# 64-wide cross attention in rounds of four steps, and tables ahead of stores in two 16-wide cross attentions

## The chip, the cores and the metric

The kernel runs on one core of one Trainium2 chip, as one launch. The metric is the device time in microseconds (us) of that core. The profile is one execution recorded by the hardware profiler. Its engines are TensorE (PE, its weight loads PEld), VectorE (DVE), ScalarE (ACT), GpSimd (POOL) and SyncE (SP), which issues the DMAs.

## The reference

Four Perceiver layers act on x (2 x 256 x 256) with a context of 2 x 4096 x 256. Each has a cross attention to the context, a self attention and a feed-forward part. The change touches the cross attentions of layers 1, 2 and 3.

```python
# layer 1: 16 heads of 64, keys and values from context and latents
q = lat @ Wq
k, v = jnp.split(jnp.concatenate([x, lat], axis=1) @ Wkv, 2, axis=-1)
attn = jax.nn.softmax(jnp.einsum('bhid,bhjd->bhij', q, k) * scale, axis=-1)
out = jnp.einsum('bhij,bhjd->bhid', attn, v)      # then @ Wout
# layers 2 and 3: 16 heads of 16
q, k, v = query @ Wq.T + bq, key @ Wk.T + bk, value @ Wv.T + bv   # split in heads, softmax as above, then @ Wo.T + bo
```

## The kernel before

Each part is a stage with a hand-written instruction list for each engine; semaphores are the only link between them. P is 128, S is 256 queries, KC and QT are 2.

**The 64-wide attention** (`latent_attention`, tiles `L1x_...`). A unit is two heads of one batch (16 units), and has 17 steps of 256 keys (34 key tiles of 128). Two steps are a pair: 136 pairs, `for p in range(PAIRS)`. A softmax needs the row maximum first, so one key tile of 512 keys and one value tile is computed per pair, some pairs ahead of its use. The PE list of a pair is

1. `first_peaks`: score products in bf16 of one key tile into banks 0 and 1 of `psm` (L1525);
2. `scores` of two steps onto banks of `pss` that hold the negated maximum already (L1542);
3. `second_peaks` into banks 1 and 2 (L1525), after DVE has read the first;
4. `tiles`: a key tile into bank 0 (L1501, L1504 for the latent's own keys), a value tile into bank 2 (L1516);
5. in 7 pairs the queries of the next group (L1482), in 15 a row of maxima spread over the partitions (`spread_rows`, L1531);
6. `average` of the two steps (L1555), and at a unit's end `denominators` (L1565).

Peaks and scores use half the array's rows (64*128 in the profile, two of them at once), tiles the whole array (128*128), averages and denominators half its columns (128*64, again two at once). So PE changes its shape three times in a pair.

The ACT list of a pair is two exponentials (L1671), two seeds that copy the maxima into `pss` (L1661), the key's copy (L1646) and the value's (L1650). DVE reads the peaks (L1730, L1733 for the latent's own), sums half of the exponentials for the denominators (L1760) and, where a unit's last peaks are in, builds the diagonal matrices of its maxima (`diagonals`, L1742 and L1747). These stand between the peaks and the sums. At a unit's end it copies the average out (`copy_out`, L1769) and normalizes (L1773, L1775). POOL sums the other half (L1464) and casts the key tile to bf16 (L1450).

**The 16-wide attentions** (`narrow_attention`, tiles `L2x_...` and `L3x_...`, 8 units each) open with a phase that PE, DVE and the DMAs share: the 64 peak tiles of unit 0 (PE L1063 by `products`, read one bank at a time by DVE at L1234) and 16 value tiles of the context (`first_values`, L1131), which ACT copies out (L1205) and SP stores (L1012) and loads again (L980). PE waits for `wv_here` ahead of the first value tile. That semaphore takes three DMAs: the weights `wv` (L997) and, behind the context's first four blocks (L990) and the stores of the query parts (L1002) in SP's list, the tables `bv` and `sel` (L1003, L1004). Then come 12 peaks of unit 1, and the unit loop with scores (L1106) and averages (L1118), which need the keys `KS` (L976) and the values `V` (L980).

## Time and profile before

| | us |
|---|---|
| median of 3 runs | 3573.69 |
| lowest, highest | 3572.43, 3589.18 |
| the profiled execution | 3585.08 |
| its span, first to last instruction | 3583.3 |
| PE, DVE, ACT, POOL busy | 3318.9, 2164.6, 1772.7, 877.4 |
| 64-wide attention (L1x), key tiles to the last denominators | 604 to 1710 |
| 16-wide attentions, start of the first peaks | 2184 (L2x), 2847 (L3x) |

The profiled execution took 11.39 us more than the median of the runs; 1.78 us of its time lie outside its span. All positions in the trace are from the span's start. A matmul's end is modelled, so PE looks busy while it changes shape; what such a change costs is seen in the distance between the starts of two groups, not in the busy time.

### The profile page before, as it was taken

Reading aid. Unit: us, or ns where it says so; the run is one execution under the profiler, and the core shown is the slowest. Engines: PE = TensorE matmul, PEld = TensorE weight load, DVE = VectorE, ACT = ScalarE, POOL = GpSimd, SP = SyncE. Lnnn points to the kernel's source line nnn. Section 1 sums busy time; section 2 is a strip of 40 time slices with the busy share of each in tenths; the row PEclk is TensorE's granted clock in tenths of the full one; section 3 lists DMA queues with packets and bytes.
Section 4 is the critical chain, followed back from the end, with each engine's and each line's share of the span. In section 5 each row is a group of like instructions: output and inputs, shape, how many; then the busy total and the mean of one; then the engine's idle time right before and its main releaser. Section 6 shows DMA issues by size and latency. Waiting matters only on the chain. (4 is left out here: it accounts for less than half of the span.)

```text
span 3583.3 us, 56143 instructions
## 1 busy us (share of the span) xinstructions
PE 3318.9 (93%) x21894; PEld 2109.8 (59%) x21894; DVE 2164.6 (60%) x3410; ACT 1772.7 (49%) x2589; POOL 877.4 (24%) x652
## 2 busy tenths in 40 slices
PE   8989898999999999999769798999988799999899
PEld 5855596666666666666436585444456544445665
DVE  4435313666666666665488405999663299984654
ACT  2325311566666666667356231677743147675621
POOL 1033000344444444445147103000030300000530
PEclk9999999999999999999889899999999999999999
DMA  5258554000001000000586426766201576650010
GB/s 190 101 176 270 198 216 160 1 10 10 1 32 35 1 10 10 1 1 1 139 308 236 158 111 181 150 120 120 49 27 37 173 180 125 120 104 23 1 70 17
DMA packets 231028, 346.79 MB, mean 97 GB/s; under 512 B 104304, under 2 KB 177712, under 8 KB 226160
## 3 DMA queue, kind: packets, MB, share of 16 engines
q1 hardware_dynamic: 230384, 342.16, 32.9%
q8 instruction: 178, 2.92, 0.3%
q0 software_dynamic: 384, 1.05, 0.1%
q14 instruction: 82, 0.67, 0.1%
HBM read 257.15 MB, written 86.02 MB: 96 GB/s over the span
## 5 line engine op out<-in xcount | busy, mean ns | idle before, releaser
L1464 POOL TENSOR_TENSOR L1x_acc<-L1x_acc,L1x_pr 128x512 f32<-128x512 f32 x256 | 357.6, 1397 | 538.6 <-ACT L1x_pr L1671 521.4
L1730 DVE TENSOR_REDUCE L1x_pk<-L1x_psm 128x2 f32<-128x1024 f32 x238 | 291.7, 1226 | 318.9 <-PE L1x_psm L1525 318.9
L1671 ACT ACTIVATE L1x_pr<-L1x_pss 128x1024 f32<-128x1024 f32 x272 | 263.7, 1021 | 300.6 <-PE L1x_pss L1542 300.5
L1234 DVE TENSOR_REDUCE L3x_pk<-L3x_psm 128x1 f32<-128x512 f32 x512 | 328.9, 685 | 23.7 <-PE L3x_psm L1063 17.3
L1234 DVE TENSOR_REDUCE L2x_pk<-L2x_psm 128x1 f32<-128x512 f32 x512 | 329.0, 685 | 23.0 <-PE L2x_psm L1063 16.6
L1211 ACT ACTIVATE L3x_pr<-L3x_pss 128x1024 f32<-128x1024 f32 x256 | 248.1, 1021 | 104.1 <-PE L3x_pss L1106 103.8
L1211 ACT ACTIVATE L2x_pr<-L2x_pss 128x1024 f32<-128x1024 f32 x256 | 248.1, 1021 | 103.0 <-PE L2x_pss L1106 102.7
L1760 DVE TENSOR_TENSOR L1x_acc<-L1x_acc,L1x_pr 128x512 f32<-128x512 f32 x256 | 275.1, 1075 | 33.5 <-ACT L1x_pr L1671 21.0
L1661 ACT COPY L1x_pss<-L1x_neg 128x1024 f32<-128x1024 f32 x272 | 278.5, 1028 | 1.3 <-DVE L1x_pk L1730 1.3
L1555 PE MATMUL L1x_pso<-L1x_pr,L1x_V 128*64 128x256 f32 x2176 | 265.3, 386 | 2.6 <-ACT L1x_pr L1671 2.6
L1501 PE MATMUL L1x_psm<-L1x_cT,L1x_w 128*128 128x512 f32 x512 | 253.4, 618 | 0.0
L1542 PE MATMUL L1x_pss<-L1x_Q,L1x_K 64*128 64x256 f32 x2048 | 244.3, 377 | 0.7 <-ACT L1x_pss L1661 0.7
L1516 PE MATMUL L1x_psm<-L1x_w,L1x_cT 128*128 128x256 f32 x1024 | 242.0, 379 | 1.3 <-DVE L1x_pk L1730 1.3
L1516 PEld LDWEIGHTS L1x_psm<-L1x_w,L1x_cT 128*128 128x128 f32 x1024 | 194.5, 190 | 79.0 <-issue 30.2
L3016 POOL TENSOR_SCALAR s_qz<-s_qT,s_mask 128x256 f32<-128x256 f32 x64 | 58.3, 920 | 657.3 <-SPq L58 437.6
L1542 PEld LDWEIGHTS L1x_pss<-L1x_Q,L1x_K 64*128 64x128 f32 x2048 | 194.5, 188 | 27.2 <-ACT L1x_pss L1661 3.7
L1555 PEld LDWEIGHTS L1x_pso<-L1x_pr,L1x_V 128*64 128x64 f32 x2176 | 143.4, 136 | 107.1 <-issue 40.7
L3998 POOL TENSOR_TENSOR o_pr<-o_h,m_cr 128x1024 f32<-128x1024 f32 x31 | 72.8, 2354 | 504.2 <-DVE o_h L4077 504.2
L841 PE MATMUL n_psk<-n_cT,n_w 128*128 128x512 f32 x256 | 126.2, 618 | 36.1 <-DMA n_cT<-in_ctxT 36.0
L1501 PEld LDWEIGHTS L1x_psm<-L1x_cT,L1x_w 128*128 128x128 f32 x512 | 87.0, 189 | 113.1 <-issue 112.8
L879 ACT ACTIVATE n_kst<-n_psk,n_b 128x512 bf16<-128x512 f32 x192 | 121.6, 688 | 57.6 <-PE n_psk L841 47.4
L1106 PE MATMUL L2x_pss<-L2x_QS,L2x_KS 97*128 97x256 bf16 x1024 | 138.1, 277 | 0.6
(747 smaller groups left out, 5881.0 us busy)
## 6 DMA issues: line engine op xcount, KB each, us to landing
f0e_wt<-in_f_pieces SPq DMA_DIRECT2D x10, 3072.0 KB, 11.5
offset_rows<-s_rows SPq DMA_DIRECT2D x32, 768.0 KB, 5.7
L2x_KS<-L2x_key_parts SPq DMA_DIRECT2D x24, 1024.0 KB, 12.9
L3x_KS<-L3x_key_parts SPq DMA_DIRECT2D x24, 1024.0 KB, 12.8
s_add<-offset_rows SPq DMA_DIRECT2D x32, 512.0 KB, 7.3
n_cT<-in_ctxT SPq DMA_DIRECT2D x32, 512.0 KB, 4.8
f1e_wt<-in_f_pieces SPq DMA_DIRECT2D x8, 2048.0 KB, 13.2
L2x_key_parts<-n_kst SPq DMA_DIRECT2D x32, 384.0 KB, 3.0
```

The source lines that it names most:

```text
L1106: i = nc.tensor.matmul(pss[:, 2 * (a % 2) + h // 2, h % 2 * S:(h % 2 + 1) * S], KS[0:ONE + 1, n % 2, h, s * P:(s + 1) * P], QS[0:ONE + 1, ...
L1211: nc.scalar.activation(pr[:, a % RING, :, :].rearrange("p h q -> p (h q)"), pss[:, 2 * (a % 2):2 * (a % 2) + 2, :].rearrange("p x q -> p ( ...
L1234: nc.vector.reduce_max(pk[:, n % 2, h * QT + qt, j:j + 1], psm[:, x % 3, :], AX).then_inc(turn_read, 1)
L1464: i = nc.gpsimd.tensor_tensor(acc[:, n, 1, :, :], acc[:, n, 1, :, :], pr[:, a % RING, :, 1, :], ALU.add)
L1501: i = nc.tensor.matmul(psm[:, x, :], w[:, g % 2, 1, c, m * P:(m + 1) * P], cT[:, c, j * 512:(j + 1) * 512], start=(c == 0), stop=(c == KC ...
L1516: i = nc.tensor.matmul(psm[:, 2, h * D:(h + 1) * D], keys, w[:, g % 2, 2, c, :], start=(c == 0), stop=(c == KC - 1))
L1542: i = nc.tensor.matmul(pss[:, 2 * (a % 2) + h, e * S:(e + 1) * S], keys, Q[half, g % 2, m, :], start=False, stop=True, skip_group_check=True)
L1555: i = nc.tensor.matmul(pso[64 * h:64 * h + 64, 0:S], V[:, (SLOTS * g + s) % VRING, e, 2 * n + h, :], pr[:, a % RING, h, e, :], start=(s == ...
L1661: nc.scalar.copy(pss[:, x:x + 2, :].rearrange("p h (e q) -> p h e q", e=2), neg[:, u % 2, :, :].unsqueeze(2).broadcast_to([P, 2, 2, S])).t ...
L1671: nc.scalar.activation(pr[:, a % RING, :, :, :].rearrange("p h e q -> p (h e q)"), pss[:, x:x + 2, :].rearrange("p h n -> p (h n)"), ACT.E ...
L1730: nc.vector.reduce_max(pk[:, m, qt, :, j], peak_banks(z, qt), AX).then_inc(peak_read, 1)
L1760: i = nc.vector.tensor_tensor(acc[:, n, 0, :, :], acc[:, n, 0, :, :], pr[:, a % RING, :, 0, :], ALU.add)
```

## The change

- **64-wide, PE.** Pairs are taken two at a time, as 68 rounds of four steps. `visit(p)` is peaks, two steps' scores, peaks; `fill(p)` is the pair's tiles. A round is `visit(2r)`, the tiles of both pairs, `visit(2r+1)`, and then four averages: those of steps 4r-2 to 4r+1. In the 10 rounds in which a unit ends ahead of the round's last step, the averages up to that end stand ahead of the tiles. In rounds without tiles (the last four) two averages follow each visit. Waits for a bank of `psm` are gathered in `bank0_free`, `bank1_free` and `bank2_free`, with counters.
- **64-wide, the others.** ACT, DVE and POOL do the work of the tiles (copies, queries, rows, casts, the end of a unit) in the even pair of the round. DVE's `diagonals` stay with the visit whose peaks complete a unit, ahead of the sums, in the even or the odd pair. One more key tile is computed ahead (`KLEAD` 12 for 11); the rings of exponentials and of values grow by two (`RING` 6, `VRING` 21). The tile `dn` goes; `rec` takes its place.
- **16-wide, peaks of unit 0.** `first_products` writes two banks and `read_first_peaks` reads both in one instruction (1024 columns for 512). The two rooms are banks 0 and 1 of `psm` and of `pss`. Four products stand ahead of one whole value tile, where two stood ahead of each half.
- **16-wide, SP.** `bv` and `sel` are issued right behind `wv`, ahead of the context's blocks and the query parts.

```diff
+        def wide_banks(x):
+            return psm[:, 0:2, :] if x % 2 == 0 else pss[:, 0:2, :]
...
             sp.dma_start(wv[:, :, :], d[pre + "_w3"][0][:, 2]).then_inc(wv_here, 16)
+            sp.dma_start(bv[:, :], d[pre + "_bvT"]).then_inc(wv_here, 16)
+            sp.dma_start(sel[:, :], d["sum_rows"]).then_inc(wv_here, 16)
             for j in range(CRING):
...
-            sp.dma_start(bv[:, :], d[pre + "_bvT"]).then_inc(wv_here, 16)
-            sp.dma_start(sel[:, :], d["sum_rows"]).then_inc(wv_here, 16)
...
+            def first_products(x):
+                if x == 0:
+                    pe.wait_ge(kh_in[0], 32)
+                    pe.wait_ge(masked, 2)
+                if x == 1:
+                    pe.wait_ge(q_act, 3 * KC)
+                if x >= 2:
+                    pe.wait_ge(wide_read, x - 1)
+                j, qt, h = peak_of(2 * x)
+                for r in range(2):
+                    i = nc.tensor.matmul(wide_banks(x)[:, r, :], QM[64 * r:64 * r + 64, 0, h, qt * P:(qt + 1) * P],
+                                         KH[64 * r:64 * r + 64, 0, j * 512:(j + 1) * 512], start=True, stop=True)
+                i.then_inc(wide, 1)
...
             for n in range(NV):
-                products(0, n * NP // NV, (2 * n + 1) * NP // NV // 2)
+                first_products(2 * n)
+                first_products(2 * n + 1)
                 if n == 0:
                     for i in range(2, 2 * NU):
                         picked(i)
                     pe.wait_ge(masked_more, NU - 1)
                     pe.wait_ge(wv_here, 48)
                 first_values(n, 0)
-                products(0, (2 * n + 1) * NP // NV // 2, (n + 1) * NP // NV)
                 first_values(n, 1)
             products(1, 0, LATE)
             rows(0)
...
+            def read_first_peaks(x):
+                j, qt, h = peak_of(2 * x)
+                dve.wait_ge(wide, x + 1)
+                nc.vector.reduce_max(pk[:, 0, h * QT + qt::2 * QT, j], wide_banks(x), AX).then_inc(wide_read, 1)
+                if x == NP // 2 - 1:
...
-    KLEAD, VLEAD, VRING, BRING = 11, 9, SLOTS + 2, 3
+    KLEAD, VLEAD, VRING, BRING = 12, 9, SLOTS + 4, 3
+    ROUNDS = ALL // 4
...
-            g, r = divmod(p, SLOTS)
-            return KC * g if r == 9 else KC * g - 1 if r == 0 and g else None
-        def averages_in(p):
-            r = p % SLOTS
-            return [2 * p] if r == 8 else [2 * p - 1, 2 * p, 2 * p + 1] if r == 9 else [2 * p, 2 * p + 1]
+            u = [completed(z) for z in (read_in(p - 1), read_in(p)) if z is not None]
+            return next((x for x in u if x), None)
+        def ends_in(r):
+            return next((u for u in range(UNITS) if 4 * r - 2 <= STEPS * (u + 1) - 1 <= 4 * r + 1), None)
+        def averages_in(r):
+            steps = range(max(0, 4 * r - 2), 4 * r + 2)
+            u = ends_in(r)
+            last = 4 * r - 1 if not filled(r) else STEPS * (u + 1) - 1 if u is not None and STEPS * (u + 1) - 1 <= 4 * r else -1
+            return [a for a in steps if a <= last], [a for a in steps if a > last]
+        def filled(r):
+            return keys_in(2 * r) is not None or values_in(2 * r) is not None
...
-                    cast(keys_in(p))
+                for q in (p, p + 1):
+                    if p % 2 == 0 and q > 0 and keys_in(q) is not None:
+                        cast(keys_in(q))
         @block.tensor
...
+            def visit(p):
                 z = read_in(p)
...
+                if z is not None:
+                    bank0_free()
+                    bank1_free()
+                    pe.wait_ge(k_cast, z + 1)
+                    peak_products(z, 0)
+                    out["read"] += 1
                 scores(2 * p)
                 scores(2 * p + 1)
-                second_peaks()
-                if p > 0:
-                    tiles()
+                if z is not None:
+                    pe.wait_ge(peak_read, QT * z + 1)
+                    if out["den"]:
+                        pe.wait_ge(den_read, out["den"])
+                    pe.wait_ge(v_ev, out["values"])
+                    peak_products(z, 1)
+            def fill(p):
+                if keys_in(p) is not None:
+                    bank0_free()
+                    key_tile(keys_in(p))
+                    out["keys"] += 1
                 if queries_in(p) is not None:
-                    pe.wait_ge(k_ev, p + KLEAD + 1)
-                    queries(queries_in(p), 0)
-                if rows_in(p) is not None:
-                    pe.wait_ge(k_ev, min(TILES, p + KLEAD + 1))
-                    spread_rows(rows_in(p), 0)
-                for a in averages_in(p):
+                    bank1_free()
+                    queries(queries_in(p), 1)
+                    out["queries"] += 1
+                if values_in(p) is not None:
+                    bank2_free()
+                    value_tile(values_in(p))
+                    out["values"] += 1
+                if p % 2 == 0 and rows_in(p) is not None:
+                    bank1_free()
+                    spread_rows(rows_in(p), 1)
+                    out["rows"] += 1
+            out = {"keys": KLEAD, "values": VLEAD, "read": KLEAD - 1, "queries": 1, "rows": 1, "den": 0}
+            for r in range(ROUNDS):
+                if r == 0:
+                    fill(0)
+                    visit(0)
+                    fill(1)
+                    visit(1)
+                else:
+                    visit(2 * r)
+                    for a in averages_in(r)[0]:
+                        average(a)
+                    fill(2 * r)
+                    fill(2 * r + 1)
+                    visit(2 * r + 1)
+                for a in averages_in(r)[1]:
                     average(a)
-                if ended_before(p) is not None:
-                    denominators(ended_before(p), min(TILES, p + VLEAD + 1))
-            denominators(UNITS - 1, TILES)
+                if ends_in(r) is not None:
+                    bank2_free()
+                    denominators(ends_in(r))
+                    out["den"] += 1
+            average(ALL - 2)
+            average(ALL - 1)
+            bank2_free()
+            denominators(UNITS - 1)
             keep_busy(nc, k, pss[:, 0, 0:P], 9)
...
                 exponentials(2 * p + 1)
                 if p + 1 < PAIRS:
                     act.wait_ge(exps, 2 * p + 1)
                     seed(2 * p + 2)
-                if p > 0 and keys_in(p) is not None:
+                if p >= 2 and not second and keys_in(p) is not None:
                     evict_keys(keys_in(p))
                 if p + 1 < PAIRS:
                     act.wait_ge(exps, 2 * p + 2)
                     seed(2 * p + 3)
-                if p > 0 and values_in(p) is not None:
-                    evict_values(values_in(p))
-                if rows_in(p) is not None:
-                    take_rows(rows_in(p), 0)
+                if not second:
+                    if p >= 2 and values_in(p) is not None:
+                        evict_values(values_in(p))
+                    if rows_in(p) is not None:
+                        take_rows(rows_in(p), 1)
+                    evict(p + 1)
             take_denominators(UNITS - 1)
...
+                    copy_out(ends_in(r - 1))
                 if z is not None:
                     read_peaks(z, 1)
                     diagonals(z)
+                if not second and ends_in(r) is not None and STEPS * (ends_in(r) + 1) <= 4 * r + 1:
+                    copy_out(ends_in(r))
                 sum_step(2 * p)
                 sum_step(2 * p + 1)
-                if p >= 1 and ended_before(p - 1) is not None:
-                    normalize(ended_before(p - 1))
-                if queries_in(p) is not None:
-                    take_queries(queries_in(p), 0)
+                if not second:
+                    for q in (p, p + 1):
+                        if queries_in(q) is not None:
+                            take_queries(queries_in(q), 1)
+                    if r >= 1 and ends_in(r - 1) is not None:
+                        normalize(ends_in(r - 1))
...
```

Before, one pair of the 64-wide attention stands in PE's list like this (`psm` and `pss` are PSUM, `Kb`, `Qb` the bf16 keys and queries, `pr` the exponentials, `cT` the context):

```order
L1525 MATMUL L1x_psm<-L1x_Kb,L1x_Qb 128x512 x2
L1542 MATMUL L1x_pss<-L1x_Q,L1x_K 128x256 x8
L1525 MATMUL L1x_psm<-L1x_Kb,L1x_Qb 128x512 x2
L1501 MATMUL L1x_psm<-L1x_cT,L1x_w 128x512 x2
L1516 MATMUL L1x_psm<-L1x_w,L1x_cT 128x256 x4
L1555 MATMUL L1x_pso<-L1x_pr,L1x_V 64x256 x8
```

The changed kernel has this round in the same place:

```order
L1560 MATMUL L1x_psm<-L1x_Kb,L1x_Qb 128x512 x2
L1577 MATMUL L1x_pss<-L1x_Q,L1x_K 128x256 x8
L1560 MATMUL L1x_psm<-L1x_Kb,L1x_Qb 128x512 x2
L1536 MATMUL L1x_psm<-L1x_cT,L1x_w 128x512 x2
L1551 MATMUL L1x_psm<-L1x_w,L1x_cT 128x256 x4
L1536 MATMUL L1x_psm<-L1x_cT,L1x_w 128x512 x2
L1551 MATMUL L1x_psm<-L1x_w,L1x_cT 128x256 x4
L1560 MATMUL L1x_psm<-L1x_Kb,L1x_Qb 128x512 x2
L1577 MATMUL L1x_pss<-L1x_Q,L1x_K 128x256 x8
L1560 MATMUL L1x_psm<-L1x_Kb,L1x_Qb 128x512 x2
L1590 MATMUL L1x_pso<-L1x_pr,L1x_V 64x256 x16
```

The instructions of two pairs are all there; the tiles stand together behind the first visit and the averages behind the second, so two pairs change shape four times where they did six times.

At the start of the 16-wide attention PE's list had, from the first peaks on (`pick` masks the queries, `wv` and `vcT` make the values):

```order
L1063 MATMUL L2x_psm<-L2x_KH,L2x_QM 128x512 x2
L1075 MATMUL L2x_pss<-L2x_qp,L2x_pick 128x512 x6
L1131 MATMUL L2x_pss<-L2x_wv,L2x_vcT 128x256 x2
L1063 MATMUL L2x_psm<-L2x_KH,L2x_QM 128x512 x2
L1131 MATMUL L2x_pss<-L2x_wv,L2x_vcT 128x256 x2
```

and now has:

```order
L1066 MATMUL L2x_psm<-L2x_KH,L2x_QM 128x512 x2
L1066 MATMUL L2x_pss<-L2x_KH,L2x_QM 128x512 x2
L1094 MATMUL L2x_pss<-L2x_qp,L2x_pick 128x512 x6
L1150 MATMUL L2x_pss<-L2x_wv,L2x_vcT 128x256 x4
L1066 MATMUL L2x_psm<-L2x_KH,L2x_QM 128x512 x2
L1066 MATMUL L2x_pss<-L2x_KH,L2x_QM 128x512 x2
```

Peaks come four at a time, in two places, and values four at a time.

SP's list at the same place, before:

```order
L997 DMA L2x_wv<-in_L2x_w 128x512
L990 DMA L2x_vcT<-in_ctxT 128x2x512 x4
L1002 DMA L2x_query_parts<-L2x_qp 128x3x512 x2
L1003 DMA L2x_bv<-in_L2x_bvT 128x4
L1004 DMA L2x_sel<-in_sum_rows 128x128
```

and now:

```order
L1001 DMA L2x_wv<-in_L2x_w 128x512
L1002 DMA L2x_bv<-in_L2x_bvT 128x4
L1003 DMA L2x_sel<-in_sum_rows 128x128
L994 DMA L2x_vcT<-in_ctxT 128x2x512 x4
L1008 DMA L2x_query_parts<-L2x_qp 128x3x512 x2
```

The two tables moved past six DMAs; the rest of SP's list is as it was.

## Rows read from the trace of the kernel before

**Rows 1.** The page: busy time of each engine over the span.
```profile
PE 3318.9 (93%) x21894; PEld 2109.8 (59%) x21894; DVE 2164.6 (60%) x3410; ACT 1772.7 (49%) x2589; POOL 877.4 (24%) x652
```
**Rows 2.** Windows: us, busy of each engine, PEclk, DMA share, GB/s; 64-wide.
```profile
720.00:1640.00 920.00, 917.59 (x5729) 584.29 (x5727) 588.74 (x602) 576.80 (x712) 411.57 (x342) 1.00 0.03 11
```
**Rows 3.** Timeline (start, length, instruction, count) of PE, one pair.
```profile
1004.08 0.39 PE L1525 MATMUL L1x_psm<-L1x_Kb,L1x_Qb 64*128 64x512 bf16 x2
1006.03 0.38 PE L1525 MATMUL L1x_psm<-L1x_Kb,L1x_Qb 64*128 64x512 bf16 x2
1006.34 1.98 PE L1501 MATMUL L1x_psm<-L1x_cT,L1x_w 128*128 128x512 f32 x4
1008.16 1.89 PE L1516 MATMUL L1x_psm<-L1x_w,L1x_cT 128*128 128x256 f32 x8
1009.98 1.95 PE L1555 MATMUL L1x_pso<-L1x_pr,L1x_V 128*64 128x256 f32 x16
1011.86 0.39 PE L1525 MATMUL L1x_psm<-L1x_Kb,L1x_Qb 64*128 64x512 bf16 x2
```
**Rows 4.** Timeline of PE: values before queries; in the lead, values before peaks.
```profile
966.10 1.89 PE L1516 MATMUL L1x_psm<-L1x_w,L1x_cT 128*128 128x256 f32 x8
967.82 1.89 PE L1482 MATMUL L1x_psm<-NT,L1x_w 128*128 128x256 f32 x8
...
614.48 1.89 PE L1516 MATMUL L1x_psm<-L1x_w,L1x_cT 128*128 128x256 f32 x8
616.31 0.60 PE L1525 MATMUL L1x_pss<-L1x_Kb,L1x_Qb 64*128 64x512 bf16 x4
```
**Rows 5.** Timeline of DVE and POOL: the sums of the pair of rows 3.
```profile
1007.60 2.39 DVE L1760 TENSOR_TENSOR L1x_acc<-L1x_acc,L1x_pr 128x512 f32<-128x512 f32 x2
...
1006.49 2.95 POOL L1464 TENSOR_TENSOR L1x_acc<-L1x_acc,L1x_pr 128x512 f32<-128x512 f32 x2 [5.55 <-ACT L1x_pr L1671]
```
**Rows 6.** Timeline of DVE, then PE, in a pair with diagonals.
```profile
973.90 1.23 DVE L1730 TENSOR_REDUCE L1x_pk<-L1x_psm 128x2 f32<-128x1024 f32 x1 [0.72 <-PE L1x_psm L1525]
975.38 2.15 DVE L1747 TENSOR_SCALAR L1x_dm<-minus_ident,L1x_mx 128x128 bf16<-128x128 bf16 x4
977.45 1.48 DVE L1760 TENSOR_TENSOR L1x_acc<-L1x_acc,L1x_pr 128x512 f32<-128x512 f32 x2
...
977.68 0.38 PE L1531 MATMUL L1x_psm<-L1x_dm,ones_bf 128*128 128x512 bf16 x1 [0.18 <-DVE L1x_dm L1747]
```
**Rows 7.** Timeline of ACT, 64-wide, two of the last pairs, without tiles.
```profile
1687.26 1.94 ACT L1671 ACTIVATE L1x_pr<-L1x_pss 128x1024 f32<-128x1024 f32 x2 [0.40 <-PE L1x_pss L1542]
1691.45 1.02 ACT L1671 ACTIVATE L1x_pr<-L1x_pss 128x1024 f32<-128x1024 f32 x1 [0.40 <-PE L1x_pss L1542]
```
**Rows 8.** Timeline of PE, 16-wide: the first values, two later ones, and L3x's first.
```profile
2194.75 2.04 PE L1131 MATMUL L2x_pss<-L2x_wv,L2x_vcT 128*128 128x256 f32 x4 [6.94 <-DMA L2x_sel<-in_sum_rows]
...
2203.90 1.13 PE L1131 MATMUL L2x_pss<-L2x_wv,L2x_vcT 128*128 128x256 f32 x4
...
2205.28 1.13 PE L1131 MATMUL L2x_pss<-L2x_wv,L2x_vcT 128*128 128x256 f32 x4
...
2857.41 2.05 PE L1131 MATMUL L3x_pss<-L3x_wv,L3x_vcT 128*128 128x256 f32 x4 [6.88 <-DMA L3x_sel<-in_sum_rows]
```
**Rows 9.** SP issues the context's blocks; the first one's landing (last column, us).
```profile
2176.49 3.46 SPq L990 DMA_DIRECT2D L2x_vcT<-in_ctxT  x4
...
L2x_vcT<-in_ctxT SPq DMA_DIRECT2D x1, 512.0 KB, 11.5
```
**Rows 10.** Issue and landing of the first values; the averages; the window's DMA share.
```profile
2247.53 0.58 SPq L980 DMA_DIRECT2D L2x_V<-L2x_values  x1
...
L2x_V<-L2x_values SPq DMA_DIRECT2D x1, 1088.0 KB, 7.3
...
2255.95 0.63 PE L1118 MATMUL L2x_pso<-L2x_pr,L2x_V 128*17 128x256 f32 x4
...
2204.00:2247.00 43.00, 39.69 (x176) 21.59 (x176) 40.14 (x64) 9.48 (x15) 0.45 (x1) 0.97 0.80 225
```

More of the change, by code:

```diff
@@ L1270, in _ @@
                 nc.vector.tensor_copy(QM[:, i // 2, 0, :], pss[:, 2, :]).then_inc(masked, 1)
-            read_peaks(0, 0, NP)
+            for x in range(NP // 2):
+                read_first_peaks(x)
             read_peaks(1, 0, LATE)
@@ new lines, in bank0_free, with bank1_free, bank2_free @@
+            def bank0_free():
+                pe.wait_ge(k_ev, out["keys"])
+                pe.wait_ge(peak_read, QT * out["read"] - 1)
+            def bank1_free():
+                pe.wait_ge(peak_read, QT * out["read"])
+                pe.wait_ge(q_ev, 2 * KC * out["queries"])
+                pe.wait_ge(row_in, out["rows"])
+            def bank2_free():
+                pe.wait_ge(peak_read, QT * out["read"])
+                pe.wait_ge(v_ev, out["values"])
+                if out["den"]:
+                    pe.wait_ge(den_read, out["den"])
@@ L1677, in take_denominators @@
                     act.wait_ge(o_done, u)
-                nc.scalar.copy(dn[:, :], psm[:, 2, 0:S]).then_inc(den_read, 1)
+                nc.scalar.copy(rec[:, :], psm[:, 2, 0:S]).then_inc(den_read, 1)
             for z in range(KLEAD):
@@ L1687, in _, with evict @@
             seed(1)
+            def evict(p):
+                if keys_in(p) is not None:
+                    evict_keys(keys_in(p))
+                if values_in(p) is not None:
+                    evict_values(values_in(p))
             for p in range(PAIRS):
+                r, second = divmod(p, 2)
                 if p == 0:
-                    evict_keys(KLEAD)
-                    evict_values(VLEAD)
-                elif ended_before(p - 1) is not None:
-                    take_denominators(ended_before(p - 1))
+                    evict(0)
+                elif not second and ends_in(r - 1) is not None:
+                    take_denominators(ends_in(r - 1))
                 exponentials(2 * p)
@@ L1783, in _ @@
                 z = read_in(p)
+                r, second = divmod(p, 2)
+                if p == 0 and queries_in(0) is not None:
+                    take_queries(queries_in(0), 1)
                 if z is not None:
                     read_peaks(z, 0)
-                if ended_before(p) is not None:
-                    copy_out(ended_before(p))
+                if not second and r >= 1 and ends_in(r - 1) is not None and STEPS * (ends_in(r - 1) + 1) > 4 * r - 3:
+                    copy_out(ends_in(r - 1))
                 if z is not None:
```

72 lines of the change are left out of this document (21 added, 51 removed).

## The prediction, made before the changed kernel was run

> **What bounds the kernel now.** I read the page first: PE is busy for 93% of the span, the next engine for 60% [rows 1]. The windows then say where that average hides something else. In the 64-wide attention PE is busy for 917.59 of 920 us at full clock, DVE and ACT for under two thirds [rows 2]: there only fewer or cheaper PE starts count. But "busy" includes what a change of the array's shape costs, so I went to the timeline of PE and took distances between starts. Two groups of one shape follow each other by 1.72 us for eight steps, 966.10 to 967.82 [rows 4], so a step is 0.2157. (A step is one 256-wide f32 or 512-wide bf16 instruction; of the half shapes, two instructions share a step.) A pair has 1+8+1+8+8+8 = 34 steps, 7.33 us, and takes 1011.86-1004.08 = 7.78 [rows 3]. The remaining 0.45 is the price of three changes:
> peaks to tiles 0.31-0.216 ahead of the first tile and 1.82-1.726 within the key tile, 0.19 together; tiles to averages 1.82-1.726 and about 0.05 inside the averages, 0.14; averages to peaks 1.88-1.726-0.05, 0.10.
> The way back from tiles to half rows, which the new order needs, stands in the lead: 1.83 for eight steps, 0.10 (614.48 to 616.31) [rows 4].
> At the start of a 16-wide attention PE instead waits 6.94 and 6.88 us for a table [rows 8], and behind that DMAs are busy for 80% of 43 us [rows 10].
>
> **64-wide, shape changes.** Of 68 rounds the first and the last four are different, 63 have tiles, and in 10 of these a unit's end puts averages between the first visit and the tiles. Two pairs before: 2 x (0.19+0.14+0.10) = 0.86, by the measured remainder 0.45 rather 0.90; I take 0.89. A plain round now has peaks to tiles 0.19, tiles to peaks 0.10, half rows to averages (not seen), averages to peaks 0.10. The unseen one lies between 0.10, the cheapest change, and 0.19, the dearest; I take 0.15, near the other way into averages (0.14). Sum 0.54, saved 0.35; 53 x 0.35 = 18.5. The ten others have half rows to averages twice, averages to tiles once (not seen, 0.10 to 0.30; I take 0.20, near the other way into tiles), tiles to peaks and averages to peaks: 0.70, saved 0.19, ten times 1.9. Together **-20 us**. The last rounds are without tiles, ACT sets their pace (4.19 a pair against 18 PE steps, 3.9, its wait 0.40 [rows 7]), and change nothing; one more pair of them has no key tile, since one more is made in the lead: **+1**.
>
> The Trainium skill says on "TensorEngine Tiling (Array Packing)", section "Key Properties", that changing the tiling mode drains TensorE, and not merely changing the tile. The 0.45 above agrees. The page gives no price; by its rule all changes may cost alike, which is the third rival.
>
> **64-wide, waits.** The short half of a round is new. Call S the start of the odd visit's second peaks. PE then has 1+16 steps and two changes, so the next first peaks start at S+3.9, and their second peaks 1.95 later (1006.03-1004.08), at S+5.8. DVE has (S = 1006.03) [rows 3, 5, 6], its second read done at S+1.57 and both sums at S+3.96. It would be wanted at S+4.3 (a read starts 0.4 behind its peaks) and, its read being 1.23 long, must begin by S+4.5. So 0.5 us of slack: no cost. The upper bound is both sums at the price beside POOL. One of the two in that group ran alone (0.74, half of 1.48 [rows 5, 6]), so the other took 1.6; two such are 3.3, DVE is free at S+4.9, and the round loses 0.4. Below zero it can't go. I take nothing, since the list of POOL, which sets it, starts at the same place as before (1006.49, S+0.46).
> With diagonals in that half it is different. They take 2.15 and start 0.25 behind the read, the sums then 1.48 [rows 6]: DVE is free at S+1.6+2.4+1.5 = S+5.5, its read ends at 6.7, PE waits to about S+6.8 for what it wanted at 5.8. That is 1.0 us, in the 7 units (of 15) whose last peaks fall in an odd pair: **+7**. In exchange the row spread finds its diagonals ready in those 7. It now waits (0.18 idle [rows 6], with the pipeline 0.25): **-2**. In the other 8 it keeps its place right behind the first tiles.
> ACT has two exponentials and two seeds in the short half, which alone take 4.19 [rows 7] of 5.8. The ring of 6 exponentials holds the four that the averages of a round take and two being made. In the long half each bank of `psm` is wanted again 3.9 us after its group's start, which has 1.8 of matmuls and a copy in it; no wait.
> 64-wide: -20+1+7-2 = **-14 us**.
>
> **16-wide, tables.** Now the first value tile waits for the tables and one block of the context. Before, the first block landed at 2176.49+11.5 = 2188.0 [rows 9], with six DMAs ahead of `sel`. Two small tables ahead of it push it to 2188.8 (0.4 each; lower bound none, upper bound half of an issue group's 3.46, 1.7). So the values start there, not at 2194.75: -5.9. The clock is low for part of this stretch, about 1 us of which goes too.
> **16-wide, wide peaks.** Two halves of a value tile start 1.38 apart [rows 8], so a tile with its four peaks takes 2.76, set by DVE's four reads. Two reads of 1024 columns are 2 x 1.23 (the same shape in L1x [rows 6]); PE has 8 value steps and 2 of peaks, 2.16 with two changes of 0.1, 2.35. DVE's 2.46 with some handover, 2.54: 16 x 0.22 = 3.5. Handover unseen: from none (2.46, 1.3 better in all) to a whole lost peak group for each tile (2.9, 5.8 worse). PE is therefore ready 9.5 us earlier, less 0.5 at the end.
> What comes behind is bound by DMAs. The values are stored and loaded again; that load is issued at 2247.53, takes 7.3, lands at 2254.8, and the averages start at 2255.95, 1.1 later [rows 10]. In 43 us the DMAs were busy for 34.4, so they can give at most 8.6. I take **-8** for each of the two attentions: **-16**. What bounds it below is the load not moving by more than half, -4 each.
>
> **The sum.** -14-16 = -30 us, against the profiled execution's 3585.08: 3555. That execution took 11.39 more than the median 3573.69, so from the median **3544**, -0.8%. What can be told from no change is 0.5%, 18 us: "faster" is below 3556, "slower" above 3592.
>
> **Rivals** (all from the median).
> - *The stores swallow the tables' gain.* The load of V moves by 4, not 8: -22, **3552**. For it: share 0.80 over the whole stretch and a single queue of loads behind stores. Against: 20% of it is free.
> - *All changes cost alike.* At 0.19 each and 0.30 for averages to tiles, a plain round saves 0.90-0.67, a split one loses 0.07: 12-1 = 11 in place of 20, so -21, **3553**. If the cost went with the groups and not with the changes, nothing is saved, 3564.
> - *Better.* DVE catches up before it is missed (the diagonals overlap the average's tail, +0 for +7) and the DMAs follow PE fully (-9.5 each): -40, **3534**.
> - *Slower: ACT is late in the odd visit.* Its exponentials now stand behind the copies of two key and two value tiles. If they start one exponential later (1.94/2 = 0.97), POOL's sums fall wholly beside DVE's: POOL's first, DVE's, POOL's, DVE's, 2 x (1.27+0.74) = 4.0 (1.27 is POOL's first sum, what 2.95 has when 0.3 of waiting and 1.4 are off), from S+0.46+0.97: DVE free at S+5.4, the second peaks 0.95 late. In 56 rounds (63 less the 7 already priced) +53: +23, **3597**. It decides from a free time of S+4.5 on, that is exponentials late by 0.07 if everything alternates, and makes the kernel slower in all from a mean stall of 0.54. Against: scores end 1.9 us behind the last tile, its copy is done by then, and ACT is only 63% busy in this stretch [rows 2].
>
> The Trainium skill, "SBUF — State Buffer", section "SBUF: two separate sides", says that a GpSimd operation and a VectorE one with two SBUF inputs hold a shared port pair as an exclusive lock, each for its whole instruction. The trace agrees so far: two sums took 1.48 alone and 2.39 beside POOL's, and by that rule the fourth rival's order of turns is how it would go.
>
> **Chances.** Main case 0.46, stores 0.15, alike 0.12, better 0.14, slower 0.08, and 0.05 that the rounds bring nothing or a wait that I don't see takes the gain (3565 to 3590). The main case's own range is 3536 to 3552 (the unseen changes 0.10 to 0.30, handover, 4 to 9 for each load). Nearly all of main, better, and most of stores and alike lie below 3556: faster 0.76, within 0.5% 0.17, slower 0.07. Holding 8 in 10 needs 3528, somewhat below "better", to 3572, which leaves out the slower case.
>
> **What would show it.** Two pairs take 15.2 us from one even first peaks to the next (15.57 before); PE idle time released by DVE of about 1 us ahead of second peaks, seven times and no more; the first values at 2188.8 less what came earlier, and about 2.54 for a value tile; the L2x averages some 8 us closer to the start of the first peaks, with V still the last to arrive. I am wrong if PE waits for DVE, or for an exponential, in most rounds; if the starts show the changes at other prices than 0.10 to 0.20; or if the averages wait for V as long as PE gained.

## The result

| | before | changed |
|---|---|---|
| median, us | 3574.53 (4 runs) | 3540.95 (4 runs) |
| lowest, highest | 3572.43, 3589.18 | 3539.25, 3542.55 |
| the profiled execution's span | 3583.3 | 3539.8 |

The ratio is 0.9897, with a 95% interval of 0.9871 to 0.9924: faster by 1.0%. Of the first result the profiles differ by 43.4 us and the medians by 33.6, so the profile has to be read by stages. From starts of the same instructions in both, in us:

| stage | before | changed | difference | forecast |
|---|---|---|---|---|
| 64-wide, first key tile to last average | 1102.3 | 1087.2 | -15.1 | -14 |
| L2x, first peaks to first average | 71.8 | 62.3 | -9.5 | -8 |
| L3x, the same | 70.9 | 62.0 | -8.9 | -8 |
| L2x, L3x, first to last average | 338.4, 339.8 | 337.3, 337.6 | -1.1, -2.2 | 0 |
| everything else | | | -6.7 | 0 |

The first three lines are what the change does, -33.5 us. 4.3 of the last line are gone before the 64-wide attention begins, in stages with the same code: the profiled execution of before was 11 us above its median.

### The profile page after: what moved, and what is told of

Its sections match the earlier page's. It is cut to its first block and busy times, and to the rows that moved or that the text cites. A ratio compares the mean times of both kernels' runs of the same rounds, so it can differ in the third digit from the quotient of the medians.

```text
span 3539.8 us, 56376 instructions
## 1 busy us (share of the span) xinstructions
PE 3283.4 (93%) x21859; PEld 2119.4 (60%) x21894; DVE 2150.0 (61%) x3346; ACT 1773.9 (50%) x2589; POOL 850.0 (24%) x652
## 5 line engine op out<-in xcount | busy, mean ns | idle before, releaser
L1253 DVE TENSOR_REDUCE L2x_pk<-L2x_psm 128x1 f32<-128x512 f32 x448 | 287.5, 685 | 13.1 <-PE L2x_psm L1082 9.4
L1253 DVE TENSOR_REDUCE L3x_pk<-L3x_psm 128x1 f32<-128x512 f32 x448 | 287.5, 685 | 10.7 <-PE L3x_psm L1082 6.9
L1590 PE MATMUL L1x_pso<-L1x_pr,L1x_V 128*64 128x256 f32 x2176 | 253.1, 383 | 0.6 <-DVE L1x_OT L1837 0.6
L1485 POOL CAST L1x_Kb<-L1x_K 128x512 bf16<-128x512 f32 x128 | 94.6, 739 | 237.3 <-ACT L1x_K L1706 237.3
```

What stands on the lines that cost most here:

```text
L1253: nc.vector.reduce_max(pk[:, n % 2, h * QT + qt, j:j + 1], psm[:, x % 3, :], AX).then_inc(turn_read, 1)
L1590: i = nc.tensor.matmul(pso[64 * h:64 * h + 64, 0:S], V[:, (SLOTS * g + s) % VRING, e, 2 * n + h, :], pr[:, a % RING, h, e, :], start=(s == ...
```

## The profile after

The page's busy line, which answers to [rows 1], and the windows, which answer to [rows 2] and to the start of the 16-wide attentions. Columns of windows: stretch, length, busy time of PE, PEld, DVE, ACT, POOL, granted clock of PE, DMA share, GB/s.

```profile
PE 3283.4 (93%) x21859; PEld 2119.4 (60%) x21894; DVE 2150.0 (61%) x3346; ACT 1773.9 (50%) x2589; POOL 850.0 (24%) x652
```

```profile
720.00:1620.00 900.00, 892.64 (x5661) 588.34 (x5673) 581.95 (x600) 576.45 (x711) 387.47 (x342) 1.00 0.03 11
2165.20:2209.00 43.80, 41.94 (x197) 26.39 (x198) 38.95 (x35) 10.55 (x18) 20.29 (x2) 1.00 0.94 286
2819.20:2865.00 45.80, 44.15 (x195) 27.06 (x196) 38.56 (x35) 10.55 (x18) 20.25 (x2) 0.93 0.92 273
```

PE is still 93% busy, of a shorter span. In the 64-wide stretch it now has 7 us of idle time in 900, where it had 2.4 in 920 [rows 2]: a little of the gain is paid back in waits. The values of the 16-wide attentions are made while the DMAs are 92 to 94% busy.

PE's timeline in a plain round, its first row the even visit's second peaks (columns: start, length, instruction, count):

```profile
1044.46 0.38 PE L1560 MATMUL L1x_psm<-L1x_Kb,L1x_Qb 64*128 64x512 bf16 x2
1044.77 1.98 PE L1536 MATMUL L1x_psm<-L1x_cT,L1x_w 128*128 128x512 f32 x4
1046.59 1.89 PE L1551 MATMUL L1x_psm<-L1x_w,L1x_cT 128*128 128x256 f32 x8
1048.32 1.88 PE L1536 MATMUL L1x_psm<-L1x_cT,L1x_w 128*128 128x512 f32 x4
1050.04 1.89 PE L1551 MATMUL L1x_psm<-L1x_w,L1x_cT 128*128 128x256 f32 x8
1051.86 0.39 PE L1560 MATMUL L1x_psm<-L1x_Kb,L1x_Qb 64*128 64x512 bf16 x2
...
1053.81 0.38 PE L1560 MATMUL L1x_psm<-L1x_Kb,L1x_Qb 64*128 64x512 bf16 x2
1054.12 3.67 PE L1590 MATMUL L1x_pso<-L1x_pr,L1x_V 128*64 128x256 f32 x32
```

The change into tiles costs 0.31-0.216 and 1.82-1.726, as in [rows 3]. The second key tile starts 1.73 behind the value tile, free of charge, and takes 1.72 where the first takes 1.82. The way back to peaks costs 0.10 (1050.04 to 1051.86), and half rows to averages 0.09 (1053.81 to 1054.12 less a step) with 0.05 inside the averages: 0.14. A plain round, from one even first peaks to the next, takes 15.22 (1138.13 to 1153.35), two pairs took 15.57.

The waits that came with it, of PE:

```profile
965.54 0.39 PE L1560 MATMUL L1x_psm<-L1x_Kb,L1x_Qb 64*128 64x512 bf16 x2 [0.24 <-DVE L1x_pk L1798]
...
994.77 1.08 PE L1599 MATMUL L1x_psm<-L1x_acc,ones_f 128*64 128x256 f32 x8 [0.31 <-DVE L1x_pk L1798]
...
998.22 0.39 PE L1560 MATMUL L1x_psm<-L1x_Kb,L1x_Qb 64*128 64x512 bf16 x2 [0.31 <-DVE L1x_pk L1798]
```

The first is the wait behind diagonals in an odd pair. Its idle time reads 0.24; from start to start it is 0.62 where 0.21 is due, 0.41. It comes 7 times in the steady part. The other two come four times each, where a unit ends at the first step of an even pair: three of the round's four averages then stand ahead of the tiles, and only one stands between the odd visit's second peaks (at S = 993.07) and the denominators. These want the bank that DVE is still reading (0.48 from start to start). DVE then has its two sums to do, and the next visit's second peaks wait for it as well (0.48 again, at S+5.15).

DVE around the first of them, to be read against [rows 6]:

```profile
959.68 1.23 DVE L1798 TENSOR_REDUCE L1x_pk<-L1x_psm 128x2 f32<-128x1024 f32 x1 [0.71 <-PE L1x_psm L1560]
960.94 0.19 DVE L1810 TENSOR_REDUCE L1x_mx<-L1x_pk 128x4 f32<-128x36 f32 x1
961.17 1.78 DVE L1815 TENSOR_SCALAR L1x_dm<-minus_ident,L1x_mx 128x128 bf16<-128x128 bf16 x4
962.87 1.47 DVE L1828 TENSOR_TENSOR L1x_acc<-L1x_acc,L1x_pr 128x512 f32<-128x512 f32 x2
964.26 1.22 DVE L1798 TENSOR_REDUCE L1x_pk<-L1x_psm 128x2 f32<-128x1024 f32 x1
```

In L2x, PE's rows that answer to [rows 8] and to the averages of [rows 10], and the landing of V:

```profile
2169.41 1.97 PE L1150 MATMUL L2x_pss<-L2x_wv,L2x_vcT 128*128 128x256 f32 x8 [0.72 <-ACT L2x_QM L1217]
...
2176.94 1.99 PE L1150 MATMUL L2x_pss<-L2x_wv,L2x_vcT 128*128 128x256 f32 x8
...
2182.03 1.99 PE L1150 MATMUL L2x_pss<-L2x_wv,L2x_vcT 128*128 128x256 f32 x8
...
2227.53 1.91 PE L1137 MATMUL L2x_pso<-L2x_pr,L2x_V 128*17 128x256 f32 x16 [2.74 <-DMA L2x_V<-L2x_values]
```

```profile
L2x_V<-L2x_values SPq DMA_DIRECT2D x1, 1088.0 KB, 10.7
L2x_values<-L2x_vvst SPq DMA_DIRECT2D x1, 544.0 KB, 6.4
```

The wait of 6.94 for `sel` is gone; 0.72 for a masked query is what is left. Two value tiles start 5.09 apart (2176.94 to 2182.03), 2.54 each. The last store takes 6.4 to land and V's load 10.7, for 7.3 in [rows 10], and PE waits 2.74 for it.

## The experiments

Nine runs, e9 of the changed kernel itself. The stage times of all of them come from their own profiles, the ratios stand against runs of the kernel before beside them.

| kernel | ratio, 95% interval | L2x, L3x: first peaks to first average | L2x, L3x: first to last average | 64-wide |
|---|---|---|---|---|
| before | 1 | 71.8, 70.9 | 338.4, 339.8 | 1102.3 |
| changed | 0.9897 (0.9871 to 0.9924) | 62.3, 62.0 | 337.3, 337.6 | 1087.2 |
| e9, the same again | 0.9905 (0.9891 to 0.9919) | 59.4, 62.6 | 338.0, 338.9 | 1087.3 |
| e3, 64-wide alone | 0.9972 (0.9962 to 0.9981) | 70.8, 72.0 | 340.2, 341.7 | 1087.2 |
| e7, both 16-wide edits | 0.9960 (0.9945 to 0.9975) | 61.2, 61.0 | 343.6, 338.0 | 1102.6 |
| e1, tables alone | 0.9964 (0.9951 to 0.9976) | 64.9, 65.5 | 338.6, 338.2 | 1102.3 |
| e2, wide peaks alone | 1.0003 (0.9992 to 1.0014) | 65.5, 67.5 | 346.9, 339.6 | 1102.6 |
| e8, e2 with 64 waits | 0.9988 (0.9977 to 0.9999) | 68.2, 67.7 | 338.3, 338.3 | 1102.4 |
| e4, tiles parted | 1.0104 (1.0081 to 1.0126) | 61.1, 63.8 | 337.0, 340.7 | 1159.6 |
| e5, a second read | 0.9920 (0.9898 to 0.9942) | 64.0, 60.8 | 338.7, 338.5 | 1093.3 |
| e6, keys earlier | 0.9892 (0.9873 to 0.9911) | 62.0, 62.0 | 337.1, 337.6 | 1087.2 |

**One part at a time: e1, e2, e3.** All three start from the kernel before. e3 takes `latent_attention` as changed and leaves `narrow_attention`; e2 is the reverse with the tables put back behind the query parts; e1 is the kernel before with

```diff
             sp.dma_start(wv[:, :, :], d[pre + "_w3"][0][:, 2]).then_inc(wv_here, 16)
+            sp.dma_start(bv[:, :], d[pre + "_bvT"]).then_inc(wv_here, 16)
+            sp.dma_start(sel[:, :], d["sum_rows"]).then_inc(wv_here, 16)
```

and the two lines taken out below.

> The kernel before with only bv and sel moved ahead of the context's blocks. My theory: in the whole change the first values started 6.4 us earlier against the first peaks (4.2 us behind them, 10.65 before), and the stretch at half clock that followed PE's 7 us wait in the kernel before (13.65 us in L2x, 10.24 in L3x) went with it, which is what made the value tiles 6.2 us shorter where 3.5 was reckoned. So with the tables alone both go: about -6.4 and -2 to -3 in each attention, the averages start 8 to 9 us earlier, the total is -16 to -18 us. Rival: the low clock belongs to this place whatever PE does; then the stretch stays and it is -6.4 each, -13 us. Second rival: the chain of loads behind it gives only part, and PE waits for V ahead of the first average: -4 to -5 each, -9 us.

> The kernel before with the wide peaks of unit 0 (two banks for a read, four products ahead of a whole value tile) and the tables still behind the query parts. My theory: 2.54 us for a value tile in place of 2.76, 3.5 us for each attention, the wait of 7 us for sel and the low clock stay: -7 us in all. Rival: DMAs behind it take it back, nothing: 0. Second rival: the wide form also shortens the stretch at half clock, since a tile then has fewer waits of PE between shapes: up to -5 each, -10.

> Only the 64-wide attention changed, the 16-wide ones as before. My theory: two pairs in 15.22 us for 15.57, with 7 waits of 0.41 us ahead of second peaks and 4 pairs of waits of 0.48 around denominators; L1x some 16 us shorter from its first key tile to the last average, total -15 to -17 us (0.9955). Rival: part of what the whole change won is due to the 16-wide ones alone and L1x is worth no more than the 11 us that equal prices of all changes gave.

e1 gave 12.6 us (3576.61 to 3563.98), 6.9 and 5.3 of them by the phase, close to my theory's wait but not its clock. The stretch at half clock did not go, it shrank (13.65 to 6.8 us in L2x, 10.24 to 6.8 in L3x). In L2x the window now reads 0.93 of the full clock:

```profile
2182.00:2232.00 50.00, 48.22 (x197) 26.16 (x198) 42.50 (x66) 10.54 (x18) 20.42 (x2) 0.93 0.91 269
```

where the kernel before had 0.88 from 2184.1 to 2240.6. Most of what went lay ahead of the first value tile: over the value tiles alone (first to last) the granted clock is 0.95 before and 0.96 in e1, and in L3x 0.95 in both. They took 45.3 us for 45.9 in L2x, 45.7 for 45.7 in L3x. So the rival on the clock was nearer. e3 gave 15.1 us in its own stage, as forecast, but only 9 in the median, and its interval of 7 to 14 leaves the 15 out. And e2 gave nothing in the median although its phase is 6.3 and 3.3 us shorter.

**Where e2's gain went: e7, e8.** The unit loop of L2x, with the same instructions, took 346.9 us for 338.4. PE's timeline in it:

```profile
2529.53 1.05 PE L1137 MATMUL L2x_pso<-L2x_pr,L2x_V 128*17 128x256 f32 x15
2533.28 0.39 PE L1137 MATMUL L2x_pso<-L2x_pr,L2x_V 128*17 128x256 f32 x1 [2.70 <-issue]
```

PE stops ahead of the last matmul of a group of 16, which waits for nothing ("issue"). In e7, which has the same PE list as e2 and other DMAs ahead, the same stands 12 us earlier at the same matmul (number 14777 of those recorded in e2, 14811 in e7, whose record has 34 or 35 more throughout):

```profile
2516.80 1.05 PE L1137 MATMUL L2x_pso<-L2x_pr,L2x_V 128*17 128x256 f32 x15
2520.82 0.61 PE L1137 MATMUL L2x_pso<-L2x_pr,L2x_V 128*17 128x256 f32 x1 [2.98 <-issue]
```

e7 takes the whole `narrow_attention` as changed; e8 adds to e2, at the end of the 64-wide attention:

```diff
+            for _ in range(64):
+                pe.wait_ge(den_read, 1)
             keep_busy(nc, k, pss[:, 0, 0:P], 9)
```

> Both edits of the 16-wide attentions (tables and wide peaks), the 64-wide one as before. In the tables alone the averages came 6.9 and 5.3 us closer to the first peaks, in the wide peaks alone 6.3 and 3.3, in the whole change 9.5 and 8.9. My theory: the two edits share the load of V and the stretch at half clock, so together they give 9.5 and 8.9, not the sums 13.2 and 8.6: -18 us for the whole kernel, give or take what the unit loops behind lose or win by PE's stops in the instruction stream (up to 8 us in the wide peaks alone). Rival: the loops' losses come from the wide peaks themselves (they fill banks and leave another state); then the loops take 3 to 8 us more here too, and the total is -10.

> The kernel with only the wide peaks, and 64 more waits in PE's list at the end of the 64-wide attention, all on a semaphore that has long passed the value, so they cost PE 1 to 3 us at most in a place where it is idle later. They only shift what stands behind them in the instruction stream. The wide peaks alone were worth nothing in total although the phase itself was 6 and 3 us shorter, since the unit loop of L2x had two stops of PE in the middle of a group of matmuls (2.68 and 3.08 us from one start to the next, released by nothing), with a stretch at half clock behind one. In kernels with the same code ahead of it such a stop stands at the same matmul, counted from the start. My theory: the stops belong to places in the stream, so here they move to other matmuls, the L2x loop takes 338 to 343 us (346.9 there), and the total falls by 3 to 8. Rival: they belong to the work (banks, keys, queues of DMAs at this time); then they stay at the same matmuls, and the total stays at 1.000.

In e8 the longest stop in these loops is 1.74 us from start to start (e2 had 3.08), the L2x loop takes 338.3 us at full clock, and the ratio goes from 1.0003 to 0.9988, at the edge of what can be told. The phase is longer than in e2 here (68.2 for 65.5 us). The windows of the loop, e2 first:

```profile
2250.50:2597.40 346.90, 335.53 (x3556) 162.21 (x3556) 307.36 (x481) 244.73 (x253) 0.00 (x0) 0.98 0.53 104
```

```profile
2255.60:2593.90 338.30, 330.40 (x3558) 161.20 (x3556) 307.50 (x481) 244.87 (x253) 0.00 (x0) 1.00 0.54 107
```

The clock is part of the loss: from 2302.81 to 2309.64 and from 2534.92 to 2538.33, beside the two long stops, it is 0.50 in e2, 10.2 us at half clock, which make up to 5 of the 8.6 us. Of e2's stops, that at 2303.2 (2.68 us) has no counterpart in e7, and of e7's that at 2258.7 (1.71 us) none in e2; so the place alone does not decide. But with 64 instructions that do no work they all moved. They go with places in the stream, not with the wide peaks. e7's rival foresaw a loop longer by 3 to 8 us from the wide peaks themselves: e7 has 5.2 in L2x, but its long stop is at e2's matmul, and the changed kernel and e9, with wide peaks, have no such loss. e7's phase is 10.6 and 9.9 us shorter; its median 13.9, midway between the 18 of the theory and the 10 of the rival. Each loop was profiled in one execution.

What PE waits for in such a stop can be read from the DMAs. The profile has a queue for instructions, and in e2 one 16 KB packet of it starts at 2530.77, in the middle of the stop that ends at 2533.28. The DMA view of 2530.7 to 2530.9 has (packets, MB, share of the DMA engines; the page has 178 such packets with 2.9 MB in all):

```profile
q8 instruction: 1, 0.02, 41.2%
```

Each of the two loops has 29 such packets in every kernel, one for some 245 matmuls and weight loads of PE (7112 in e2's loop). In the 11 profiles PE stops inside a group for over 0.9 us from start to start 27 times in these loops, and each time it goes on 2.5 to 3.0 us behind the start of such a packet. With packets some 11.7 us apart this is no chance: PE waits there for a block of its instructions. At most packets it does not stop; why a few come late is not shown, and no run changes how instructions are loaded.

**The changed kernel again: e9.**

> The changed kernel once more, beside the two others. The ratio should be 0.990 (0.9897 before), and its L2x values phase, which in the first profile had no stretch at half clock (39.7 us from the first to the last value tile), should be at 41.3 to 41.7 if that was luck of one execution, as in the two later kernels with the same code there, or at 39.7 again if it belongs to the kernel.

0.9905, and the L2x values again without a stretch at half clock (granted clock 1.00):

```profile
2170.70:2214.60 43.90, 42.04 (x197) 26.47 (x198) 39.06 (x35) 10.55 (x18) 18.59 (x2) 1.00 0.90 272
```

39.7 us from the first to the last value tile, twice; e4, e5, e6 and e7, with the same PE list in this phase, have 41.3 to 41.7, L3x 41.3 to 41.8. The clock is all of that difference. The phase's length times its granted clock is 39.6 to 39.7 us in all 16 phases with wide peaks (41.7 x 0.95 in the changed kernel's L3x), and 43.4 to 43.5 in the 6 without (45.3 x 0.96 in e1's L2x). So wide peaks are worth 3.8 us for each attention at full clock, where 3.5 were forecast, and the rest is whether a stretch at half clock falls into the phase. What decides that I can't say. Twice in the same kernel speaks for the kernel, but with one execution of each luck is not ruled out.

**Changes of shape by themselves: e4.** Two averages go between the tiles of the two pairs, in the 53 plain rounds:

```diff
                     fill(2 * r)
+                    early = averages_in(r)[1][:2] if plain(r) else []
+                    for a in early:
+                        average(a)
                     fill(2 * r + 1)
```

> The changed kernel, but in the 53 plain rounds the first two of the four averages stand between the tiles of the first pair and those of the second: peaks, tiles, averages, tiles, peaks, averages. The same instructions, six changes of shape for four. If the cost goes with the changes: tiles to averages 0.14 and averages to tiles about 0.20 more for each round, less nothing: +0.34 x 53 = +18 us against the changed kernel, two pairs at 15.56. If the cost went with the groups or with the length of a run of one shape: 0 to +5. If leaving the averages for tiles were as dear as the upper bound 0.30: +23.

It cost 74 us, four times what I had written. PE's timeline, a round and the next visit (S, as in the prediction, is the start of the odd visit's second peaks, here 1188.37):

```profile
1174.99 0.39 PE L1563 MATMUL L1x_psm<-L1x_Kb,L1x_Qb 64*128 64x512 bf16 x2
...
1179.08 1.89 PE L1554 MATMUL L1x_psm<-L1x_w,L1x_cT 128*128 128x256 f32 x8
1180.89 1.95 PE L1593 MATMUL L1x_pso<-L1x_pr,L1x_V 128*64 128x256 f32 x16
1182.77 1.98 PE L1539 MATMUL L1x_psm<-L1x_cT,L1x_w 128*128 128x512 f32 x4
1184.59 1.89 PE L1554 MATMUL L1x_psm<-L1x_w,L1x_cT 128*128 128x256 f32 x8
...
1188.37 0.38 PE L1563 MATMUL L1x_psm<-L1x_Kb,L1x_Qb 64*128 64x512 bf16 x2
1188.68 1.95 PE L1593 MATMUL L1x_pso<-L1x_pr,L1x_V 128*64 128x256 f32 x16
1190.56 0.39 PE L1563 MATMUL L1x_psm<-L1x_Kb,L1x_Qb 64*128 64x512 bf16 x2
1190.79 1.92 PE L1580 MATMUL L1x_pss<-L1x_Q,L1x_K 64*128 64x256 f32 x16
1193.52 0.39 PE L1563 MATMUL L1x_psm<-L1x_Kb,L1x_Qb 64*128 64x512 bf16 x2 [0.82 <-DVE L1x_pk L1805]
```

From even first peaks to even first peaks it is 1190.56-1174.99 = 15.57, against 15.22: the two more changes cost 0.35, where I had written 0.34. Averages to tiles are 0.20 (1.88 for eight steps, of which 0.05 inside, and 1.82 for the next eight). That settles the price. But I had overlooked what the two averages did where they were: they stood in the short half and gave DVE its time. Without them the next second peaks are due at S+4.1 and start at S+5.15, 1.0 us late by 1193.52-1190.79 = 2.73 for 1.73. A round then takes 16.59, 1.37 more, and 53 of them are 73 us, the whole loss.

**How much slack the short half has: e5.** In the odd pair the second peaks are read once more, into a spare tile, ahead of the real read:

```diff
                 if j < NBLK:
+                    if twice:
+                        nc.vector.reduce_max(spare[:, z // 2, :], peak_banks(z, qt), AX)
```

> The changed kernel with one more read of the second peaks on DVE (1.23 us, into a spare tile) in the odd pair of each round, where the read is of 512-wide blocks; the output is the same. It doses the short half of the round. My theory: DVE has about 0.6 us of slack there (free at S+3.96 and wanted at S+4.5 to 4.6), so a round loses 1.23-0.6 = 0.6 us, in some 56 rounds 35 us, and in the 7 with diagonals the whole 1.2, 9 us: +40 to +45 us against the changed kernel. Rival: DVE's place in the short half doesn't bound anything (the second peaks of the next visit may be late while ACT or POOL set the pace, or PE catches up): under +10. Second rival: there is no slack at all, and the sums are pushed wholly beside POOL's: +1.2 a round, +75.

It cost 6.1 us in the 64-wide stage and 5 to 8 by the ratios, not 40. DVE in such a half (S = 1010.61):

```profile
1011.03 1.23 DVE L1800 TENSOR_REDUCE L1x_spare<-L1x_psm 128x2 f32<-128x1024 f32 x1 [0.71 <-PE L1x_psm L1561]
1012.17 1.22 DVE L1801 TENSOR_REDUCE L1x_pk<-L1x_psm 128x2 f32<-128x1024 f32 x1
1013.31 1.82 DVE L1831 TENSOR_TENSOR L1x_acc<-L1x_acc,L1x_pr 128x512 f32<-128x512 f32 x2
1015.04 1.22 DVE L1801 TENSOR_REDUCE L1x_pk<-L1x_psm 128x2 f32<-128x1024 f32 x1
```

The two sums, pushed 1.1 us back and so partly beyond POOL's, take 1.82 in place of 2.39. The next read starts at S+4.43, 0.55 later than the S+3.88 that it could have had, and not 1.2. In e4 the second peaks came 1.27 behind the start of DVE's read at S+3.88; those of the changed kernel are due at S+5.87, so the read may start as late as S+4.60. The slack is 0.7 us, and this dose does not use it up. Most of what it cost stands at unit ends: four denominators come 1.6 us late for 0.5, in exchange the 0.5 behind each goes, and three more come 0.7 late; 1 us lies in the first rounds. The 9 us that I had written for the diagonals did not come either, at most 0.1 each for 1.2. Pushed back beyond POOL's sums, the four diagonals take 0.74 in place of 1.78, which takes back 1.0 of the 1.2:

```profile
964.59 0.74 DVE L1818 TENSOR_SCALAR L1x_dm<-minus_ident,L1x_mx 128x128 bf16<-128x128 bf16 x4
```

**The store behind the keys: e6.**

```diff
-                if NCH - CRING <= j < NCH - 1:
-                    stack(0, [j - NCH + CRING])
+                if 2 <= j < 5:
+                    stack(0, [j - 2])
```

> The changed kernel with the three key loads KS of unit 0 issued two places earlier in SP's list (behind the stores 2, 3 and 4 of the values, not 4, 5 and 6), in both 16-wide attentions. In the changed kernel PE waits 2.74 us for V ahead of the first average, and the last store (issued at 2210.13, landed 6.4 us later) stands behind the third key load. My theory: the last store then lands some 3 us after its issue, V's load is issued and lands 2.5 to 3 us earlier, the wait of 2.74 nearly goes: -2.5 for each attention, -5 us against the changed kernel. Rival: the key loads now delay the context's blocks and the stores that hold the ring, PE waits for these instead: 0 or slower. Second rival: V is late because DMAs are saturated in all of the stretch, whatever the order: 0.

V was no longer waited for:

```profile
2226.61 0.61 PE L1082 MATMUL L2x_psm<-L2x_KH,L2x_QM 64*128 64x512 bf16 x2
2227.15 1.70 PE L1137 MATMUL L2x_pso<-L2x_pr,L2x_V 128*17 128x256 f32 x16
```

and yet the phase is only 0.3 us shorter in L2x and not at all in L3x: L2x had its stretch at half clock here, 41.6 us for the values against 39.7. 0.9892 can't be told from 0.9897 and 0.9905. In L3x of the changed kernel PE had not waited for V at all, so there was nothing to win. No kernel here is faster than the changed one by more than the interval.

## Why the prediction was right, step by step

- **Shape changes, -20.** Right in size and cause: a plain round is 0.35 us shorter, and a split one into which no wait falls 0.20, for 0.19 reckoned. The round of 15.22 was forecast; half rows to averages, not seen before, cost 0.14 (taken 0.15), averages to tiles 0.20 (taken 0.20), and e4 put two changes back for 0.35. The rival in which all cost alike (the second, which the prediction once calls the third) is out.
- **Diagonals in the short half, +7.** The mechanism and the count of 7 are right, the size is not: 0.41 each, 3 us. The read starts at S+5.0 (964.26, S = 959.26) and not at S+5.5. Most of that is the term of 2.15 for the diagonals, which take 1.78 where POOL has no cast behind its sums; the rest is what the prediction rounded up.
- **Row spread, -2.** Right. In e9, whose record has these matmuls, the 7 with diagonals in an odd pair start 0.22 behind the matmul ahead of them, the others 0.56, as all did before: 7 x 0.35 = 2.4.
- **Not foreseen:** the four unit ends at which one average is left for the short half, 4 x 0.96 = 4 us. The prediction gave every short half its four averages, although three stand ahead of the tiles in these rounds. It is e4's wait: the next second peaks start at S+5.15 in both (998.22 with S = 993.07). That this cancels what the diagonals were overpriced by is luck.
- **DVE in the short half otherwise, 0.** Right, with 0.7 us of slack for the 0.5 forecast. e4 shows the wait that would have come with less work of PE in that half: 1.0 us a round. The slower rival, in which ACT is late, did not come; POOL's and DVE's sums have the times of [rows 5].
- **Tables, -5.9.** The first values start 4.22 and 4.65 us behind the first peaks for 10.65 and 10.17: -6.4 and -5.5. They wait last for a masked query (0.72), neither for the tables nor for the context's block that the prediction had.
- **Wide peaks, 2.54 a tile.** 2.54 measured; 3.8 us for the phase at full clock, 3.5 reckoned.
- **The chain behind, -8 of 9.5.** It was -9.5 and -8.9, in e9 -12.4 and -8.3, in e7 -10.6 and -9.9. In L2x PE was ready 12.2 us earlier, and not 9.5: 2.4 of that is half clock that fell away in the values; the prediction names 1 us for the clock and has none of it in the 9.5. 2.74 of it went into waiting for V, as the rival on the stores had it in kind; its -4 is too small a gain.
- **The sum.** -33.5 in the three stages against -30. Total -33.6 and -32 in the medians (e9). The parts by themselves give less: e3 8.9 and e7 13.9 in the medians, 23 together, with intervals of some 3 and 5 us to either side. In their profiles the unit loops lost 3.7 (e3) and 3.4 us (e7) against the kernel before, while those of the changed kernel won 3.3 (e9 1.3). That would be 8 to 10 of the missing 10, which with these intervals is itself at the edge of what can be told. But it is one execution each, and what no kernel here changes (the span less the stages of the table) took anything from 1648 us (e5) to 1663 (e9), 1653 in the changed kernel's first profile. So where the 10 are stays open. The stages bear the mechanism out; that the total came within 4 us of the forecast is partly luck.

## What to carry to other kernels

Price a change of the array's shape from distances between starts, for each pair of shapes, and then count the changes in a round: here they cost 0.10 to 0.20 us each, and fewer of them gave some 20 us, with no instruction removed. When groups are merged, one stretch between two rendezvous of PE and another engine gets longer and another shorter; ask of the short one what the other engine still has to do in it, in every kind of round, the four rare ones too. And when one part is measured alone, read its own stage in the trace: stops elsewhere that move with the length of the list were as large as the gain. Where the clock differs between two profiles, compare length times granted clock.

## What had not been expected of the hardware

PE stops for 1.3 to 3.4 us from start to start in the middle of a group, in 22 of 27 cases released by nothing that the profile shows (in the others it names ACT), mostly at the same matmul in kernels with the same PE list ahead of it, whatever the time. In the changed kernel, e4, e5, e6 and e9 each loop has one, of 1.4 to 1.7 us, at the same matmul. 64 idle waits put ahead took away the long ones (e8). All 27 end 2.5 to 3.0 us behind the start of a 16 KB packet of the instruction queue.

DVE's small operations feel POOL more than its sums do. The four bf16 diagonals (128x128) take 0.74 to 0.76 us where POOL's sums are over or in their last 0.3 us, and 1.7 to 2.2 where one has just begun; in these the first takes 1.2 to 1.3 us, ending 0.05 behind POOL's sum, a second 0.6 where a cast of POOL follows, and the others 0.24. Here are four in e4, to set beside 1.78 above and 2.15 in [rows 6]:

```profile
1130.17 0.76 DVE L1822 TENSOR_SCALAR L1x_dm<-minus_ident,L1x_mx 128x128 bf16<-128x128 bf16 x4
```

The Trainium skill ("SBUF — State Buffer", section "SBUF: two separate sides") says that the port pair which VectorE and GpSimd share is held for a whole instruction by whoever starts first, where VectorE's operation runs in a two-port mode or has two inputs in SBUF. The trace agrees: one operation of the four bears the wait for one of POOL's. It also fits e5, where sums and diagonals that begin later cost less.
